# Longer rows for the heads, routing between expert products, and a tail in four groups

## The reference

```python
x = x + _layernorm(_L0_attn_ref(_layernorm(x), ...))   # 16 heads of 16, rotary, softmax over 2048 keys
x = x + _layernorm(_L0_ffn_ref(_layernorm(x), ...))    # 16 experts, 2 of them for a row, and a shared expert
x = x + _layernorm(_L1_attn_ref(_layernorm(x), ...))   # gated delta rule, 32 value heads
x = x + _layernorm(_L1_ffn_ref(_layernorm(x), ...))    # dequantised gated feed-forward

# _L0_ffn_ref, the layer that most of the change is in
logits = jnp.einsum('th,eh->te', x, gate_w)
scores = jax.nn.softmax(logits, axis=-1)
topk_w, topk_idx = jax.lax.top_k(scores, K)                      # K = 2
combine = jnp.sum(jax.nn.one_hot(topk_idx, E) * topk_w[..., None], axis=1)
gu = jnp.einsum('th,ehj->etj', x, w_gate_up)
h = _swiglu(gu, I)                                               # I = 176
y = jnp.einsum('eti,eih,te->th', h, w_down, combine)
gu_s = x @ shared_gate_up                                        # shared expert, width 352
y = y + _swiglu(gu_s, SI) @ shared_down
```

## Time and profile before

| | |
|---|---|
| median of 3 runs | 3926.74 us |
| profiled execution | 3922.44 us |
| its span | 3920.7 us |
| mean granted clock of PE | 0.953 |
| busy share PE, DVE, ACT, POOL | 91%, 73%, 61%, 49% |
| DMA | 149.25 MB, mean 38 GB/s |

### The profile page before, as it was taken

How to read it: one execution, slowest core, us unless ns; L and a number is a source line. 1 busy time by engine, 2 the same in 40 slices (tenths; PEclk the granted TensorE clock), 3 DMA queues, 4 the chain that set the end, 5 groups by cost and what they waited for, 6 DMA issues and landing times. The chain is left out here.

```text
span 3920.7 us, 69538 instructions
## 1 busy us (share of the span) xinstructions
PE 3557.1 (91%) x22894; PEld 2220.4 (57%) x22894; DVE 2846.2 (73%) x6749; ACT 2405.8 (61%) x6468; POOL 1915.3 (49%) x4634
## 2 busy tenths in 40 slices
PE   6699999997896259999999999999999999999789
PEld 3133333333553237777777777777777777777645
DVE  4688888883322457888888888888888888888543
ACT  1066666666132057777777777777777777777411
POOL 3100000001302148777777777777777777777300
PEclk9599999999798589999999999999999999999989
DMA  6500000004123011111111111111111111111010
GB/s 156 98 1 1 1 1 1 1 1 165 70 63 89 11 38 30 40 29 33 39 40 30 32 39 30 40 37 23 40 40 28 32 40 38 31 32 29 13 39 17
DMA packets 204306, 149.25 MB, mean 38 GB/s; under 512 B 148739, under 2 KB 185731, under 8 KB 200752
## 3 DMA queue, kind: packets, MB, share of 16 engines
q1 hardware_dynamic: 200880, 136.42, 13.5%
q0 software_dynamic: 3072, 8.39, 0.7%
HBM read 102.69 MB, written 41.68 MB: 37 GB/s over the span
## 5 line engine op out<-in xcount | busy, mean ns | idle before, releaser
L2109 POOL TENSOR_TENSOR dl_blocks_tmp<-dl_blocks_l,dl_blocks_x 128x60 f32<-128x60 f32 (+24 forms) x1984 | 713.7, 360 | 305.7 <-DMA dl_blocks_l<-lm_dram 169.6
L2114 POOL TENSOR_TENSOR dl_blocks_x<-dl_blocks_x,dl_blocks_tmp 128x60 f32<-128x60 f32 (+24 forms) x1984 | 701.7, 354 | 155.4
L632 DVE TENSOR_REDUCE part_max<-mx 128x1 f32<-128x512 f32 x1024 | 636.5, 682 | 81.9 <-PE mx L494 81.8
L568 ACT ACTIVATE normed_t<-sc 128x1024 f32<-128x1024 f32 x512 | 496.5, 1021 | 222.2 <-PE sc L505 222.0
L2266 DVE SCALAR_TENSOR_TENSOR dl_conv<-dl_raw,dl_weights,dl_conv 128x512 f32<-128x512 f32 x768 | 581.2, 784 | 27.7 <-ACT dl_conv L2037 23.2
L1808 PE MATMUL prep<-normed_t,dl_weights 128*128 128x512 f32 x1024 | 482.8, 595 | 19.5 <-DMA dl_weights<-in_w_delta 17.3
L494 PE MATMUL mx<-k_t,q_t 96*128 96x512 bf16 x1024 | 375.1, 401 | 23.3 <-PEq L182 14.6
L475 POOL COPY v_staged<-v 128x256 f32<-128x256 f32 x16 | 6.3, 400 | 704.7 <-PE o_ps L517 704.6
L1967 ACT ACTIVATE dl_q_state<-rec_a,t_neg_decay 128x128 f32<-128x128 f32 x512 | 159.8, 365 | 240.0 <-DVE dl_r L2171 240.0
L505 PE MATMUL sc<-q_t,k_t 99*128 99x512 bf16 x1024 | 305.6, 381 | 0.6
L517 PE MATMUL o_ps<-normed_t,v_staged 128*32 128x512 f32 x2048 | 272.8, 605 | 0.4 <-ACT normed_t L568 0.4
(11 more groups left out here) (303 smaller groups left out, 7792.6 us busy)
## 6 DMA issues: line engine op xcount, KB each, us to landing
dl_blocks_l<-lm_dram SPq DMA_DIRECT2D x256, 128.0 KB, 2.7
dl_weights<-in_w_delta SPq DMA_DIRECT2D x16, 1032.0 KB, 4.9
lm_dram<-dl_lm SPq DMA_DIRECT2D x256, 32.0 KB, 1.7
xs_dram<-dl_blocks_x SPq DMA_DIRECT2D x64, 128.0 KB, 2.5
dl_inverse_t<-xs_dram SPq DMA_DIRECT2D x256, 32.0 KB
qk_dram<-hd_parts SPq DMA_DIRECT2D x48, 128.0 KB
rows_dram<-moe_zeros SPq DMA_DIRECT2D x1, 6016.0 KB, 23.1
moe_x_rows<-rows_dram SPq DMA_DIRECT2D x47, 128.0 KB, 2.2
```

Source lines behind the costliest of these rows:

```text
L568: act.activation(probs[:, e % 2, u * 2 * BQ:(u + 1) * 2 * BQ], flat(sc[u][:, :, :]), ACT.Exp, scale=float(DH) ** -0.5).then_inc(s["exp_don ...
L632: dve.reduce_max(part_max[:, t % NT, x[2]:x[2] + 1], bank_of(x)[:, :], AX.X).then_inc(s["ring_read"], 1)
L2109: pool.tensor_tensor(out, L[:, 0:i, i].unsqueeze(1).broadcast_to([P, NM - c0, i]), Xs[:, c0:NM, i:i + 1].broadcast_to([P, NM - c0, i]), AL ...
L2114: pool.tensor_tensor(Xs[:, c0:NM, 0:i], Xs[:, c0:NM, 0:i], out, ALU.add).then_inc(s["solve_step"], 1)
```

## The change

1. The parts' DRAM array is ordered part, feature, head, row, so a returned row is one stretch of 32 KB. What is written, in what pieces and when, and the three transfers of a return stay.
2. The routing's instructions on DVE, the two rank products on PE and Exp on ACT are cut into pieces that stand between the units of the shared expert.
3. The gathers, the combination and both norms stand in the expert block, in four groups; the second gathered row goes into the space of the expert weights, and the block of `norm_phase` is gone. Normalisation is on ACT instead of DVE.

The diff, cut to its core: SP's list of the head phase; the space for the tail; POOL's root and its order with the gathers; PE's and ACT's loops over the units; ACT's order at the end; DVE's pieces behind unit u; DVE's order at the end; the block that goes; the array.

```diff
-                    sp.dma_start(a["qk_dram"][side, u, :, part, :, BT * b:BT * b + BT],
+                    sp.dma_start(a["qk_dram"][side, u, part, :, :, BT * b:BT * b + BT].rearrange("d h t -> h d t"),
...
-                    sp.dma_start((QT, KT)[side][DH * band:DH * (band + n), HALF * u:HALF * u + HALF, :],
-                                 a["qk_dram"][side, u, :, first:first + n, :, :].rearrange("h c d t -> (c d) h t")
+                    sp.dma_start(flat((QT, KT)[side][DH * band:DH * (band + n), HALF * u:HALF * u + HALF, :]),
+                                 a["qk_dram"][side, u, first:first + n, :, :, :].rearrange("c d h t -> (c d) (h t)")
...
+        spare = wdn[:, :, :, :].rearrange("p e j d -> p (e j d)")
+        back = (normed[:, :, :], wgu[:, 0, :, :].rearrange("p e n -> p (e n)")[:, 0:NT * D].rearrange("p (t d) -> p t d", t=NT))
+        scaled_rows = [spare[:, r * NT * D:(r + 1) * NT * D].rearrange("p (t d) -> p t d", t=NT) for r in range(2)]
...
+        RANK_UNIT = 6
+        EXP_UNIT = 6
...
+            def root(r, g):
+                k = number[r, g]
+                at = slice(PER * g, PER * g + PER)
+                pool.wait_ge(var_done, was["var_done"] + k + 1)
+                pool.tensor_scalar(rstd[r][:, at], mv[r][:, at, 1], LN_EPS, None, ALU.add)
+                pool.tensor_scalar(shift[r][:, at], mv[r][:, at, 0], -1.0, None, ALU.mult).then_inc(rstd_done, 1)
...
+            gather(0)
+            gather(1)
+            root(0, 0)
+            gather(2)
+            root(0, 1)
+            root(1, 0)
+            gather(3)
+            root(0, 2)
...
             for u in range(N_U + 2):
+                if u == RANK_UNIT:
+                    rank_rows()
+                if u == 2:
+                    pe.wait_ge(s["link"], 1)
...
+            for g in range(GROUPS):
+                pe.wait_ge(scaled, was["scaled"] + number[1, g] + 1)
...
+                if u == EXP_UNIT:
+                    act.wait_ge(s["shifted"], 1)
+                    act.activation(flat(scores[:, :, :]), flat(logits[:, :, :]), ACT.Exp)
...
+            normalise(0, 0)
+            normalise(0, 1)
+            normalise(1, 0)
+            copy(0)
...
+                if u == 0:
+                    best_scores()
+                if u == 1:
+                    best_experts()
+                if u == 3:
+                    choices()
+                if u == RANK_UNIT:
+                    ranks()
+                if u == RANK_UNIT + 1:
+                    row_counts()
+                if u == RANK_UNIT + 2:
+                    tile_ends()
+                if u == RANK_UNIT + 3:
+                    slots()
+                if u == RANK_UNIT + 4:
+                    tile_experts()
+                if u == RANK_UNIT + 6:
+                    weights()
...
+            for r, g in ORDER:
+                if r == 0:
+                    combine(g)
+                    spread(0, g, c.Y)
+                else:
+                    add(g)
+                    dve.wait_ge(added, was["added"] + g + 1)
+                    spread(1, g, c.X)
...
-            norm_phase(c, "ln2", True)
...
-    aps["qk_dram"] = nc.dram_tensor("qk_dram", (2, 2, HEADS // 2, 3, DH, T), BF16).ap()
+    aps["qk_dram"] = nc.dram_tensor("qk_dram", (2, 2, 3, DH, HEADS // 2, T), BF16).ap()
```

More of the change, by code:

```diff
@@ L891, in moe_phase @@
         gathered = [c.sem(ctx, f"moe_gathered{i}") for i in range(GROUPS)]
+        stats_done, var_done, rstd_done, scaled, added, turned, copied, _ = c.norm.values()
+        was = dict(c.counted)
+        PER = NT // GROUPS
+        ORDER = [(0, 0)]
+        for g in range(GROUPS):
+            ORDER += [(0, g + 1)] * (g + 1 < GROUPS) + [(1, g)]
+        number = {x: i for i, x in enumerate(ORDER)}
+        for name, n in (("stats_done", 2 * GROUPS), ("var_done", 2 * GROUPS), ("rstd_done", 6 * GROUPS + 1),
+                        ("scaled", 2 * GROUPS), ("added", GROUPS), ("turned", NT // 2), ("copied", NT // 2)):
+            c.counted[name] += n
+        RANK_UNIT = 6
+        EXP_UNIT = 6
+        tp = [x[:, :].rearrange("p (j k c) -> p j k c", j=2, k=KD) for x in xt_ps]
         block = ctx.enter_context(nc.Block())
@@ L1032, in _ @@
                     down(u - 2)
+            for g in range(GROUPS):
+                pe.wait_ge(scaled, was["scaled"] + number[1, g] + 1)
+                for i in range(2 * g, 2 * g + 2):
+                    if i >= 2:
+                        pe.wait_ge(copied, was["copied"] + i - 1)
+                    for j in range(2):
+                        for k in range(KD):
+                            last = pe.transpose(tp[i % 2][:, j, k, :], scaled_rows[1][:, 2 * i + j, k * P:(k + 1) * P],
+                                                c.ident[:, :])
+                    last.then_inc(turned, 1)
         @block.scalar
         def _(act):
-            act.wait_ge(s["shifted"], 1)
-            act.activation(flat(scores[:, :, :]), flat(logits[:, :, :]), ACT.Exp)
-            act.activation(flat(top[:, :, :]), flat(top[:, :, :]), ACT.Exp).then_inc(s["exped"], 1)
             def copy_x(u):
@@ L1068, in _, with normalise, copy @@
                     copy_y(u - 2)
+            def normalise(r, g):
+                act.wait_ge(rstd_done, was["rstd_done"] + 3 * number[r, g] + 4)
+                src = (c.Y, c.X)[r]
+                for t in range(PER * g, PER * g + PER):
+                    last = act.activation(scaled_rows[r][:, t, :], src[:, t, :], ACT.Identity, bias=shift[r][:, t:t + 1],
+                                          scale=rstd[r][:, t:t + 1])
+                last.then_inc(scaled, 1)
+            def copy(g):
+                for i in range(2 * g, 2 * g + 2):
+                    act.wait_ge(turned, was["turned"] + i + 1)
+                    act.activation(c.XT[:, :, 2 * i * P:(2 * i + 2) * P].rearrange("p k (j c) -> p j k c", j=2),
+                                   tp[i % 2], ACT.Copy).then_inc(copied, 1)
+            normalise(0, 0)
+            normalise(0, 1)
+            normalise(1, 0)
+            copy(0)
+            normalise(0, 2)
+            normalise(1, 1)
+            copy(1)
+            normalise(0, 3)
+            normalise(1, 2)
+            copy(2)
+            normalise(1, 3)
+            copy(3)
         @block.vector
@@ L1096, in _ @@
[L1096 to L1130, removed]
@@ new lines, in combine, with spread @@
+            def combine(g):
+                dve.wait_ge(gathered[g], 16 * 2 * PER)
+                dve.wait_ge(s["y_copied"], PER * g + PER)
+                for k in range(2):
+                    for t in range(PER * g, PER * g + PER):
+                        last = dve.scalar_tensor_tensor(c.Y[:, t, :], back[k][:, t, :], top[:, t, k:k + 1], c.Y[:, t, :],
+                                                        ALU.mult, ALU.add)
+                    linked(last)
+            def spread(r, g, src):
+                for t in range(PER * g, PER * g + PER):
+                    last = dve.bn_stats(stats[r][:, t, :], src[:, t, :])
+                last.then_inc(stats_done, 1)
+                dve.wait_ge(stats_done, was["stats_done"] + number[r, g] + 1)
+                for t in range(PER * g, PER * g + PER):
+                    last = dve.bn_aggr(mv[r][:, t, :], stats[r][:, t, :])
+                last.then_inc(var_done, 1)
```

109 lines of the change are left out of this document (83 added, 26 removed).

## The result

The changed kernel took 3883.3 us (median of 4 runs, 3880.64 to 3885.24) beside 3927.4 for the kernel before, a ratio of 0.9889 with a 95% interval of 0.9878 to 0.9901: 44.1 us less, with the whole interval below 1. The forecast was 3883.0. The execution profiled took 3883.3 us too; its span is 39.1 us shorter than that of the earlier trace rows.

What follows compares the result with a forecast made beforehand. It took the head as bound by row returns, the expert stage by PE waiting for routing, and the tail as 95.2 us without products. 3922.4 - (2 + 16.5 + 25) + 4.3 gave 3883 us; 8-in-10 range 3854 to 3895.

Steps and rivals of the forecast that it cites:

- Rows of 32 KB: Head phase: one 32 KB piece per returned row instead of eight of 4 KB gains 2 us in all.
- The 0.7 us a return: Head phase: estimated gain per return from fewer pieces, a thirtieth of 21.9 us.
- Rivals 1 and 2: Head: long pieces free the return, 15 to 43 us gain (chance 0.20), or slow it, 3949 us (0.04).
- rival 4: Head: hardware cuts 32 KB rows into shorter pieces, head keeps its time, 3885 us; chance counted within the forecast's 0.63.
- Routing: Expert stage: moving routing between products removes PE's waits and a slow-clock stretch, 16.5 us (16.0 to 18.0).
- the 0 to 2 us for table loads: Expert stage: allowance for Exp between two Silus costing ACT two more table loads of 1.28 us.
- the 5.74 us of work on ranks and first products: Expert stage: PE's work before the change, taken as all at 1.2 GHz, part of 8.1 us at full clock.
- rival 3: Expert stage: routing stays on the path by delaying PE or the scatter; 8 to 12 us lost, 3891 to 3895; chance 0.13.
- Tail: First gather to last copy: gather, combination and norms in four groups take 70 us instead of 95.2, gain 25.
- The 4.3 us added for the median: Whole kernel: the median shown, 3926.74, stood 4.3 us above the profiled execution, so this was added to the forecast.
- Ports: Head: by the skill's port rule, a return takes 19.3 us whatever the piece; gain at most 2.6 us each, 8 in all.
- The shared port: Tail: if gathers count as SBUF readers, two DVE additions hold POOL 2.4 us, making the tail 72.4 instead of 70.

Runs made afterwards that it cites:

- e1: Kernel before with only the returned rows as one 32 KB piece instead of eight of 4 KB: 3923.25 us, ratio 1.0000.
- e2: Kernel before, 4 KB pieces, with each return's three transfers on partitions 48 to 95, 16 to 47 and 0 to 15: 3914.46 us, ratio 0.9976.
- e5: Changed kernel (32 KB rows) with the return's transfers on other partitions, the same edit as e2: 3877.93 us, ratio 0.9874.
- e6: The e5 kernel with each return's second and third transfer issued from ACT's queue instead of SP's: 3871.32 us, ratio 0.9855.

## Why the prediction was right

*Rows of 32 KB*, 2 us: no gain that can be told from zero. The 0.7 us a return did not come: returns land after 22.5 to 23.6 us in the changed kernel, 22.7 to 23.3 before (e1). The reason for expecting little held: partitions, not pieces (e1, e2, e5). The three periods together moved attention by less than the head varies between executions (144.7 to 146.5 us with the old rows, 145.1 to 149.5 with the new). Rivals 1 and 2 fall with e1; rival 4 falls with the packet count.

*Routing*, 16.5 us: 17.7 by the stage (18.0 alone), near the upper bound. The clock's lower level held for 5 us behind the gate products, less than the 5.7 assumed as the least, and the 0 to 2 us for table loads were not needed: PE has no wait around the rank products. One reading was off: the 5.74 us of work on ranks and first products were not all at 1.2 GHz, their window before has a granted clock of 0.60:

```profile
1005.84:1011.58 5.74, 5.74 (x12) 3.54 (x12) 3.35 (x13) 0.65 (x2) 0.00 (x0) 0.60 0.00 0
```

So the work at full clock was 8.7 us instead of 8.1; with 5 us at the lower level that gives 17.7, and the two errors nearly cancel. Slots at 1030.44 (1030 forecast), fetch at 1072.88 (1073) and first fetched row at 1084.17 (1084) agree better than was earned, since this execution's gate products ended 1.7 us later than before; behind their end it is 29.3, 71.7 and 83.0 us for 30.5, 73.5 and 84.5. With 9.9 us spare (9) rival 3 found nothing to delay.

*Tail*, 25 us: 25.3, with 47.0 us between first and last gather (47), the first combination of the last group 49.8 behind the first gather (48.5 to 51.5) and 69.9 in all (70).

*The sum.* Stages: 17.7 + 25.3, and the head's 1.1 if it counts, 43.0 to 44.1 us; forecast 43.5. That they meet to half a microsecond is luck in part: routing gave 1.2 us more than its term, and the rows' 2 us are not there. Against the profiled execution the gain is 39.1, since the stage ahead of the gate took 2.8 us more and what follows the last copy some 2. Over 13 profiles with the same code that stage runs from 50.7 to 54.2 us, and the profile of before had one of the short ones; what follows the last copy, the same code too, runs from 2582.6 to 2590.0. The 4.3 us added for the median covered this; that was an offset of runs, not a term that was understood.

*Ports.* The at most 2.6 us a return of the Trainium skill's page "SBUF — State Buffer" (Door 1: The DMA port swizzle) did not come: no rate in the trace changed with the piece. Its mapping of partitions told the direction of e2 and overstated the size: 4.8 us sooner for the first transfer by it, 3.5 to 4.0 measured.

*The shared port.* By the rows above, two gathers began 0.60 and 0.37 us after an addition had begun. They took 1.41 and 1.65 us instead of 0.95, and both ended 0.82 us behind the addition's end. So POOL was held to the end of the addition, which agrees with the Trainium skill's page "SBUF — State Buffer" (Who interferes with whom). The 2.4 us of the prediction would have needed both gathers to begin with the additions; as they fell, 1.2 us were lost, and the tail stayed at 70.

## What to carry to other kernels

If a transfer's rate differs between parts of equal piece length, change where they land before how they are cut. A return that nobody needs yet belongs behind the work that ends the phase: that one move of order was worth 14 us where longer pieces were worth none. And where executions differ by 5 to 10 us, measure a change of 2 to 4 us as the length of its own stage in the trace.

## What the runs showed of the hardware

On partitions 48 to 95 the first transfer of 1.573 MB landed 10.1 to 11.8 us after its issue (medians, e2 and e5), against 14.1 to 15.1 on 0 to 47 (before and after); three times the rate of 16 partitions would have been 5.3 us for the transfer itself. What holds it there is open: the piece does not (e5), and sending the other two transfers by another queue did not shorten the return (e6).

A gather that began beside an addition of two tiles on DVE ended 0.81 to 0.87 us behind the addition's end, in all nine kernels with the new tail (its length alone is 0.95), so what it lost was what was left of the addition, less some 0.13 us. One that had begun before the addition kept its 0.94 to 0.96 us.
